# Linear attention in row and column groups of the TensorE array, numerators and denominators taken transposed

## What is computed

```
q, k, v = jnp.split(x @ Wqkv.T + bqkv, 3, axis=-1)          # each [B, L, H, E], H = 16 heads, E = 32
q = (jax.nn.elu(q) + 1.0 + FEAT_EPS) / jnp.sqrt(E)
k = jax.nn.elu(k) + 1.0 + FEAT_EPS
kv_cumsum = jnp.cumsum(jnp.einsum('blhe,blhf->blhef', k, v), axis=1)
k_cumsum = jnp.cumsum(k, axis=1)
num = jnp.einsum('blhe,blhef->blhf', q, kv_cumsum)
den = jnp.einsum('blhe,blhe->blh', q, k_cumsum)[..., None] + FEAT_EPS
out = (num / den).reshape(B, L, D) @ Wout.T + bout           # then a layer norm and the residual
```

## Time and profile before

| what | value |
|---|---|
| median of 3 runs | 1418.9 us (1415.56 to 1419.02) |
| the profiled execution's own time | 1421.52 us |
| span in its trace | 1419.4 us |
| TensorE | 1324.6 us busy, 93% of the span |
| VectorE | 774.0 us, 55% |
| ScalarE | 632.2 us, 45% |
| GpSimd | 392.0 us, 28% |
| granted TensorE clock, mean | 0.981 |

### The profile page before, as it was taken

How to read it: one execution, slowest core, us unless ns; L and a number is a source line. 1 busy time by engine, 2 the same in 40 slices (tenths; PEclk the granted TensorE clock), 3 DMA queues, 4 the chain that set the end, 5 groups by cost and what they waited for, 6 DMA issues and landing times. The chain is left out here.

```text
span 1419.4 us, 27453 instructions
## 1 busy us (share of the span) xinstructions
PE 1324.6 (93%) x7110; PEld 1020.0 (72%) x7111; DVE 774.0 (55%) x1808; ACT 632.2 (45%) x1320; POOL 392.0 (28%) x314
## 2 busy tenths in 40 slices
PE   5999999999999999999997888999999999999991
PEld 4888878888888878788886544676677676677670
DVE  4445565565655655655655354665655566655540
ACT  3443344353343433443532114466666566656650
POOL 0001020030030210200300303455555555756441
PEclk9999999999999999999999988999999999999996
DMA  5721110201111101101002105799999999999985
GB/s 199 281 98 32 31 48 17 62 16 39 38 32 31 46 16 31 47 16 54 24 1 71 56 23 208 220 324 324 339 297 303 267 339 306 358 289 314 265 219 87
DMA packets 67184, 204.71 MB, mean 144 GB/s; under 512 B 16047, under 2 KB 18351, under 8 KB 56768
## 3 DMA queue, kind: packets, MB, share of 16 engines
q1 hardware_dynamic: 43248, 159.71, 31.3%
q0 software_dynamic: 23888, 44.40, 14.9%
HBM read 177.26 MB, written 37.03 MB: 151 GB/s over the span
## 5 line engine op out<-in xcount | busy, mean ns | idle before, releaser
L370 POOL TENSOR_TENSOR rstd<-vep,half 128x1 f32<-128x1 f32 x32 | 17.8, 555 | 600.4 <-DVE vep L537 600.3
L856 PE MATMUL bank<-ch,wkh 128*128 128x256 f32 x512 | 160.6, 314 | 8.1 <-DVE cl L548 8.0
L458 ACT ACTIVATE kt<-bank,colb 128x256 f32<-128x256 f32 x128 | 60.5, 472 | 239.1 <-PE bank L858 238.8
L1494 PE MATMUL ebank<-guh,xth 128*128 128x512 f32 x380 | 154.7, 407 | 1.6 <-DVE xtl L1387 1.0
L1382 DVE TENSOR_TENSOR gul<-wgu,guh 128x2048 fp32r<-128x2048 f32 x54 | 123.8, 2293 | 55.3 <-ACT guh L1299 48.4
L1496 PE MATMUL ebank<-guh,xtl 128*128 128x512 f32 x380 | 149.0, 392 | 0.0
L1495 PE MATMUL ebank<-gul,xth 128*128 128x512 f32 x380 | 148.3, 390 | 0.0
L1229 POOL DMA_INDIRECT xg<-xn_rows,ig x95 | 121.3, 1277 | 85.1 <-issue 71.2
L858 PE MATMUL bank<-ch,wkl 128*128 128x256 f32 x512 | 144.3, 282 | 0.0
L857 PE MATMUL bank<-cl,wkh 128*128 128x256 f32 x512 | 144.2, 282 | 0.0
L1524 PE MATMUL ebank<-wd,ht 128*128 128x512 f32 x292 | 134.4, 593 | 0.8 <-ACT ht L1284 0.8
(11 more groups left out here) (247 smaller groups left out, 2817.2 us busy)
## 6 DMA issues: line engine op xcount, KB each, us to landing
wgu<-in_egu SPq DMA_DIRECT2D x54, 1024.0 KB
wd<-in_edn SPq DMA_DIRECT2D x54, 512.0 KB
sgu<-in_egu SPq DMA_DIRECT2D x17, 1024.0 KB
craw<-in_ctx SPq DMA_DIRECT2D x32, 514.0 KB, 3.2
sdn<-in_edn SPq DMA_DIRECT2D x17, 512.0 KB
wqkv<-in_wqkv SPq DMA_DIRECT2D x1, 3072.0 KB, 18.4
second_sums<-x1b SPq DMA_DIRECT2D x9, 256.0 KB, 3.7
xa<-in_x SPq DMA_DIRECT2D x8, 256.0 KB, 2.7
```

What stands on the lines that cost most here:

```text
L856: mm(out, wkh[:, c, w], h[:, c, :], start=c == 0, stop=False)
L1494: mm(out, ah[:, c, :], bh[:, c, :], start=c == 0, stop=False)
```

## The change

The features of q are written once, dense, to `qp` (one DVE instruction over 128 partitions). A is computed by 16 small matmuls for a tile, each over the 32 rows of one head: weights `kp[r, g, :]` (32 x 128), moving `qp[r, g, :]` (128 columns). Heads of row groups i0 and i0 + 1 alternate, one bank for each row group, so A0 and A1 are done in one piece, and A2 and A3 in another. Numerators and denominators are taken transposed, with features on partitions: the weights are now 32 columns wide (`ones` for the denominators in OUTa, the head's values in OUTb), the moving operand is the masked `am[:, i, w]` of the head (128 columns), and the result goes to the 32 partitions of column group i. OUTa holds the denominators of all heads, each repeated on 32 partitions, OUTb the numerators. DVE adds the epsilon and takes reciprocals over the whole 128 x 512 denominators, and multiplies OUTb by them into `ott`. The step oT goes, with its transposes and ScalarE's copy. With one step fewer, outproj, x3T, router and pos change banks.

```diff
--- before.py
+++ after.py
@@ -65,7 +65,7 @@
 
 
 POST = {6: ["oproj"], 9: ["x1T"], 10: ["q", "k"], 11: ["v"], 14: ["A0", "A1"], 15: ["A2", "A3"], 16: ["OUTa"], 17: ["OUTb"],
-        18: ["oT"], 19: ["outproj"], 22: ["x3T", "router"], 23: ["pos"]}
+        19: ["outproj"], 22: ["x3T", "router"], 23: ["pos"]}
 SHA = 4
 SHARED = {0: [("xT", 0), ("xT", 1)], 2: [("gu", 0)], 4: [("hT", 0)], 5: [("down", 0)], 6: [("gu", 1)], 9: [("xT", 2)], 11: [("hT", 1), ("down", 1)],
           17: [("xT", 3)], 19: [("gu", 2), ("gu", 3)], 22: [("hT", 2), ("hT", 3)], 23: [("down", 2)]}
@@ -149,10 +149,9 @@
         am = sb("am", [P, DC, D])
         mn, mxx = am[:, 0:2, :], am[:, 2:4, :]
         kp = x2[:, :].rearrange("p (c n) -> p c n", c=DC)
-        qz = raw[:, :, :].rearrange("p c (i n) -> p c i n", i=HG)
-        ve = sb("ve", [P, NH, HD + 1])
-        rd = sb("rd", [P, 2, NH // 2])
-        o = xn[:, :].rearrange("p (h e) -> p h e", h=NH)
+        qp = raw[:, 0, :].rearrange("p (c n) -> p c n", c=DC)
+        ve = sb("ve", [P, D])
+        rd = xn
         lg = sb("lg", [P, E])
         v8, i8, f8 = sb("v8", [P, K]), sb("i8", [P, K], U32), sb("f8", [P, K])
         e8, w8, wsum = sb("e8", [P, K]), sb("w8", [P, K]), sb("wsum", [P, 1])
@@ -493,9 +492,6 @@
                 if n in ("x1T", "x3T"):
                     px_wait(act, n, t)
                     nc.scalar.copy(xt[:, :, :], out[:, :].rearrange("p (c n) -> p c n", c=DC)).then_inc(done, 1)
-                if n == "oT":
-                    px_wait(act, n, t)
-                    nc.scalar.copy(ott[:, :, :], out[:, :].rearrange("p (c n) -> p c n", c=DC)).then_inc(done, 1)
                 if n in ("q", "k"):
                     j = "qk".index(n)
                     wait(act, s_mn, 2 * t + j + 1)
@@ -523,7 +519,6 @@
             V = nc.vector
             V.memset(y[:, :], 0.0).then_inc(s_zero, 1)
             V.memset(msum[:, :], 0.0)
-            V.memset(ve[:, :, HD:HD + 1], 1.0)
             dve.drain()
             V.memset(rs[:, :], 0.0).then_inc(s_zero, 1)
 
@@ -626,7 +621,6 @@
                     dve.wait_ge(s_vlps, 1)
                     V.tensor_tensor(vlc[:, :, :], px[0][:, 0:DC * NB].rearrange("p (c n) -> p c n", c=DC),
                                     colb[:, 2, :].unsqueeze(2).to_broadcast([P, DC, NB]), ALU.add).then_inc(s_vlsb, 1)
-                    V.memset(qz[:, :, :, :], 0.0)
                     dve.drain()
                 if k == 4 and front:
                     if b < 3 or nxt:
@@ -679,30 +673,26 @@
                     dve.drain()
                     wait(dve, s_e, 2 * (t + 1))
                     wait(dve, s_ys, 16 * t)
-                    for i in range(HG):
-                        r = slice(i * HD, (i + 1) * HD)
-                        V.scalar_tensor_tensor(qz[r, :, i, :], mn[r, 0, :].rearrange("p (c n) -> p c n", c=DC), FEAT_EPS,
-                                               mxx[r, 0, :].rearrange("p (c n) -> p c n", c=DC), ALU.add, ALU.add)
+                    V.scalar_tensor_tensor(qp[:, :, :], mn[:, 0, :].rearrange("p (c n) -> p c n", c=DC), FEAT_EPS,
+                                           mxx[:, 0, :].rearrange("p (c n) -> p c n", c=DC), ALU.add, ALU.add)
                     V.scalar_tensor_tensor(kp[:, :, :], mn[:, 1, :].rearrange("p (c n) -> p c n", c=DC), FEAT_EPS,
                                            mxx[:, 1, :].rearrange("p (c n) -> p c n", c=DC), ALU.add, ALU.add).then_inc(s_phi, 1)
                     px_wait(dve, n, t)
-                    V.tensor_tensor(ve[:, :, 0:HD], out[:, :].rearrange("p (h e) -> p h e", h=NH),
-                                    rowb[:, 1, :].rearrange("p (h e) -> p h e", h=NH), ALU.add).then_inc(done, 1)
+                    V.tensor_tensor(ve[:, :], out[:, :], rowb[:, 1, :], ALU.add).then_inc(done, 1)
                 if n[0] == "A":
                     g = int(n[1])
                     px_wait(dve, n, t)
                     V.tensor_tensor(am[:, g, :].rearrange("p (i n) -> p i n", i=HG), out[:, :].rearrange("p (i n) -> p i n", i=HG),
                                     causal.unsqueeze(1).to_broadcast([P, HG, P]), ALU.mult).then_inc(done, 1)
-                if n[:3] == "OUT":
-                    j = "ab".index(n[3])
-                    hv = out[:, 0:8 * (HD + 1)].rearrange("p (h e) -> p h e", h=8)
+                if n == "OUTa":
                     px_wait(dve, n, t)
-                    V.tensor_scalar(rd[:, j, :], hv[:, :, HD], FEAT_EPS, None, ALU.add)
-                    dve.drain()
-                    V.reciprocal(rd[:, j, :], rd[:, j, :])
-                    dve.drain()
-                    V.tensor_tensor(o[:, 8 * j:8 * j + 8, :], hv[:, :, 0:HD], rd[:, j, :].unsqueeze(2).to_broadcast([P, 8, HD]),
-                                    ALU.mult).then_inc(done, 1)
+                    V.tensor_scalar(rd[:, :], out[:, :], FEAT_EPS, None, ALU.add).then_inc(done, 1)
+                    dve.drain()
+                    V.reciprocal(rd[:, :], rd[:, :])
+                    dve.drain()
+                if n == "OUTb":
+                    px_wait(dve, n, t)
+                    V.tensor_tensor(ott[:, :, :].rearrange("p c n -> p (c n)"), out[:, :], rd[:, :], ALU.mult).then_inc(done, 1)
                 if n == "outproj":
                     px_wait(dve, n, t)
                     V.tensor_tensor(xn[:, :], out[:, :], rowb[:, 2, :], ALU.add).then_inc(done, 1)
@@ -926,15 +916,12 @@
                     wait(pe, s_xn, 2 * t + 2)
                 if n == "A0":
                     wait(pe, s_phi, t + 1)
+                if n in ("A1", "A3"):
+                    return
                 if n == "OUTa":
-                    for g in range(DC):
-                        m = f"A{g}"
+                    for m in ("A2", "A3"):
                         wait(pe, s_xe[BANK[m]], t * PER[BANK[m]] + NTH[m] + 1)
-                    wait(pe, s_xe[BANK["v"]], t * PER[BANK["v"]] + NTH["v"] + 1)
-                if n == "oT":
-                    for m in ("OUTa", "OUTb"):
-                        wait(pe, s_xe[BANK[m]], t * PER[BANK[m]] + NTH[m] + 1)
-                before = {"outproj": "oT", "router": "x3T"}.get(n)
+                before = {"outproj": "OUTb", "router": "x3T"}.get(n)
                 if before:
                     wait(pe, s_xe[BANK[before]], t * PER[BANK[before]] + NTH[before] + 1)
                 if n == "pos":
@@ -957,16 +944,25 @@
                     for c in range(DC):
                         last = mm(out[:, :], xt[:, c, :], wqkv[:, c, 2 * D:3 * D], start=c == 0, stop=c == DC - 1)
                 elif n[0] == "A":
-                    g = int(n[1])
-                    last = mm(out[:, :], kp[:, g, :], qz[:, g, :, :].rearrange("p i n -> p (i n)"), start=True, stop=True)
+                    i0 = int(n[1])
+                    second = f"A{i0 + 1}"
+                    wait(pe, s_xe[BANK[second]], t * PER[BANK[second]] + NTH[second])
+                    pe.sem_inc(tick, 1)
+                    for g in range(DC):
+                        for i in (i0, i0 + 1):
+                            r = slice(i * HD, (i + 1) * HD)
+                            ins = mm(px[BANK[f"A{i}"]][:, g * P:(g + 1) * P], kp[r, g, :], qp[r, g, :], start=True, stop=True)
+                            if g == DC - 1:
+                                ins.then_inc(s_px[BANK[f"A{i}"]], 1)
+                    return
                 elif n[:3] == "OUT":
-                    for i in range(8):
-                        h = 8 * "ab".index(n[3]) + i
-                        last = mm(out[:, i * (HD + 1):(i + 1) * (HD + 1)], am[:, h // HG, (h % HG) * P:(h % HG + 1) * P], ve[:, h, :],
-                                  start=True, stop=True)
-                elif n == "oT":
-                    for c in range(DC):
-                        last = tr(out[:, c * P:(c + 1) * P], xn[:, c * P:(c + 1) * P], ident)
+                    pe.sem_inc(tick, 1)
+                    for g in range(DC):
+                        for i in range(HG):
+                            w = slice(g * P, (g + 1) * P)
+                            h = g * HG + i
+                            last = mm(out[i * HD:(i + 1) * HD, w], ones[:, 0:HD] if n == "OUTa" else ve[:, h * HD:(h + 1) * HD], am[:, i, w],
+                                      start=True, stop=True)
                 elif n == "outproj":
                     for c in range(DC):
                         last = mm(out[:, :], ott[:, c, :], wout[:, c, :], start=c == 0, stop=c == DC - 1)
```

## The result

The changed kernel takes 1396.57 us (median of 4, 1395.45 to 1400.45) where the kernel before took 1417.68 in the same job: a ratio of 0.9855, 95% interval 0.9832 to 0.9877. It is faster by some 21 us. I had forecast 9 us, with 1399 as the lower end of the range; the rival "more than pairs", at 1397 and a chance of 0.08, was what happened.

The account below looks back on a forecast made before the run. TensorE's passes bound seven tiles, the chain's latency the tail. Passes -16.9, edges +4.8 and tail +3.0 gave -9.1 us: 1412.4 against the profiled 1421.52, 1410 for the measurement, range 1399 to 1446.

Parts of the forecast that it names:

- more than pairs: Rival: in TensorE's new pieces, passes of three or four column groups overlap, -21.6 us in all, 1397 us; chance 0.08.
- What bounds it: Whole kernel: tiles 0 to 6 cost the sum of TensorE's passes (busy 97.57 of 100 us), the tail its chain's latency.
- The passes after: TensorE, steady tiles: A's 32 and OUT's 64 passes of 128 columns, overlapping in pairs, save 16.9 us over seven tiles.
- The edges: TensorE, changes between small-group and full-size pieces: eight a tile, four priced at 0.17 us; 0.7 us a tile, 4.8 in seven.
- The transposes and their wait: TensorE, oT in steady tiles: four passes, 0.43 us, plus 0.27 us waiting for VectorE's last multiply, all saved.
- Sum of a tile: TensorE, steady tile: 7.55 us before; over seven tiles, passes -16.9 us and shape changes +4.8 us.
- VectorE: Steady tile: held 4.8 us behind OUTa, 3.98 of it the reciprocal; idle time covers it, cost zero, about 1 us reserve.
- The tail: Tile 7's post work alone: output projection begins 1.8 us later and runs 1 us longer at lower clock; +3.0 us.

## Why the prediction was wrong, step by step

- **What bounds it**: right. Seven tiles by TensorE's passes, one tail by its chain.
- **The passes after** is the step that failed: "in a queue that starts matmuls in order this gives one matmul for each 0.107 us, not four: 48 x 0.107 = 5.14 us". That is the wait of the second pass, which the forecast made everything behind it share. The queue does not start matmuls in order across groups (runs with four of a group in a row, two in a row, and A's row groups one at a time): while a second pass waits for its group, passes of the other groups start. A came out nearly as said, since there are only two groups to share, 32 passes in 1.9 us; OUT's 64 took 1.7 instead of 3.42. Together they are 3.6 us, next to the 3.42 of the lower bound, which stood in the text as the far end. Of the Trainium skill's "TensorE: Matmul & The Clock Gate", Part 3, I took the sentence that matmuls keep their order and left out the factors, 3.07 for four row groups and 2.38 for three column groups. On the order the runs differ from the page: second passes are overtaken. On the factor they lie above it: 0.107 / 0.026 = 4.1 for four column groups, within a piece and without its edges.
- **The edges**: 0.7 us a tile predicted, 1.4 measured (0.34 a pair, run with a full-size matmul between). The bound of 0.17 for one was right, and my choice of four edges where there are eight was not: with all eight the sum of a tile closes (below). The Trainium skill, "TensorEngine Tiling (Array Packing)", Key Properties, says that every change of the tiling mode drains TensorE; the trace agrees for the pair that was measured. Between one column-group piece and the next there is none.
- **The transposes and their wait**: 0.70 us a tile, gone as said.
- **Sum of a tile**: 7.55 to 3.6 + 1.4 would be 2.6 less; the tile lost 2.7. Forecast was 1.7. The faster passes outweigh the dearer edges, so the two errors partly cancel.
- **VectorE**: the reciprocal took 3.35 us for 3.98, 6.2 ns for each further number, where my slope from 4 to 8 numbers gave 7.5. The estimate of 8.3 ns from the eight repeats in the Trainium skill, "VectorE: DVE Perf Modes", First, the fixed hardware budget, was higher still. No cost in steady tiles, right; the place where it would first have hurt was wrong.
- **The tail**: +3.0 predicted, +1.1 measured. 0.6 of the difference is the reciprocal, and the output projection did not slow down: 5.40 us, where the earlier trace rows had 5.85. The pieces before it paid instead: OUTa and OUTb took 1.93 and 1.96 us for 1.08, at a granted clock of 0.50 from 801.96 to 805.50, behind 1.35 us without work.

## What to carry to other kernels

Here the passes of four heads of 32 in four column groups cost the time of one, because neighbours in the queue sit in different groups: turn the loops so that the group index is the innermost. Price a piece in small groups as (passes / groups) x one pass plus 0.34 us for going in and out. Putting such pieces side by side saves at most that: here 0.2 us a tile. Many small instructions in a loop's body can cost more than they save by being fetched; look at the packets of the instruction queue and at stops without a releaser behind the loop's turn. And before two medians are compared to a few microseconds, look whether a stop that is not the change's stands in one of the profiles.

## What the runs showed of the hardware that I had not expected

- A pass whose group is busy lets passes of other groups by; each group has three places to wait (starts of 0.81, 0.85 and 2.19 us for one, two and four matmuls of a group in a row).
- Passes of 32 columns in column groups start 0.009 us apart on average, 64 in 0.76 us.
- With a longer loop body the instruction queue moved 69 packets instead of 27, 9 in one tile of the loop where the changed kernel had none, and a tile took 102.4 us in the loop and 93.9 ahead of it.
- A reciprocal over 512 numbers for each partition takes 3.35 us, over 8 it takes 0.20.
